# Routed experts: gate matmuls turned round, row scatters in one run, and another order of fetches and weight splits on ScalarE

## The reference

```
logits = einsum('bsh,he->bse', x, gate_w)
topv, topi = top_k(logits, 2)
w = softmax(topv, axis=-1)
w_e = einsum('bske,bsk->bse', one_hot(topi, 8), w)
out = einsum('bsh,eho,bse->bso', x, expert_w, w_e)
x = x + out
```

## Time and profile before

| | |
|---|---|
| runs | 1197.5, 1197.85, 1200.87 us; median 1197.85 us |
| profiled execution | 1197.45 us, its span 1195.6 us |
| TensorE busy | 1056.4 us (88%) |
| TensorE weight loads busy | 856.5 us (72%) |
| VectorE busy | 716.7 us (60%) |
| ScalarE busy | 359.7 us (30%) |
| GpSimd busy | 528.7 us (44%) |
| mean granted TensorE clock | 0.902 of full |

### The profile page before, as it was taken

How to read it: one execution, slowest core, us unless ns; L and a number is a source line. 1 busy time by engine, 2 the same in 40 slices (tenths; PEclk the granted TensorE clock), 3 DMA queues, 4 the chain that set the end, 5 groups by cost and what they waited for, 6 DMA issues and landing times. The chain is left out here.

```text
span 1195.6 us, 23715 instructions
## 1 busy us (share of the span) xinstructions
PE 1056.4 (88%) x8870; PEld 856.5 (72%) x8870; DVE 716.7 (60%) x1535; ACT 359.7 (30%) x828; POOL 528.7 (44%) x569
## 2 busy tenths in 40 slices
PE   6677766799999978999999999999999999873993
PEld 3344444688888767888888888888888887662782
DVE  5789999554444467566556556556656666640424
ACT  3544553222222233222222222222222222312331
POOL 0655666133213345545445444544544442045545
PEclk9767775699999988999999999999999999855997
DMA  8980000312101012110101101110110000035767
GB/s 313 394 268 2 0 2 2 76 46 75 53 26 47 27 35 63 48 34 28 53 28 46 36 27 45 29 52 27 27 54 27 28 10 1 26 131 184 219 199 251
DMA packets 61601, 90.88 MB, mean 76 GB/s; under 512 B 10376, under 2 KB 23944, under 8 KB 61512
## 3 DMA queue, kind: packets, MB, share of 16 engines
q1 hardware_dynamic: 51912, 68.09, 17.9%
q10 hardware_dynamic: 6624, 12.06, 3.1%
q0 software_dynamic: 2976, 9.44, 2.5%
HBM read 54.45 MB, written 35.13 MB: 75 GB/s over the span
## 5 line engine op out<-in xcount | busy, mean ns | idle before, releaser
L115 PE MATMUL PS<-NTh,W 128*128 128x256 f32 (+2 forms) x688 | 216.7, 315 | 0.0
L116 PE MATMUL PS<-NTl,W 128*128 128x256 f32 (+2 forms) x688 | 213.9, 311 | 0.0
L117 PE MATMUL PS<-NTh,W 128*128 128x256 f32 (+2 forms) x688 | 213.8, 311 | 0.0
L116 PEld LDWEIGHTS PS<-NTl,W 128*128 128x128 f32 (+1 forms) x688 | 131.2, 191 | 7.0
L117 PEld LDWEIGHTS PS<-NTh,W 128*128 128x128 f32 (+1 forms) x688 | 129.2, 188 | 8.5
L115 PEld LDWEIGHTS PS<-NTh,W 128*128 128x128 f32 (+1 forms) x688 | 129.4, 188 | 7.1
L1433 POOL TENSOR_TENSOR W<-ca_raw,W 128x512 fp32r<-128x512 f32 x64 | 82.5, 1291 | 114.8 <-ACT W L1283 114.8
L1371 DVE TENSOR_REDUCE ca_su<-room 128x4 f32<-128x256 f32 x64 | 26.9, 420 | 155.4 <-ACT room L1299 155.4
L1400 DVE TENSOR_TENSOR room<-PS,ca_sinT 64x512 f32<-64x512 f32 (+1 forms) x192 | 115.1, 600 | 2.6
L115 PE MATMUL PS<-W,ca_aTh 128*128 128x512 f32 x256 | 108.1, 422 | 3.2 <-DVE X L1388 3.1
L117 PE MATMUL PS<-W,ca_aTl 128*128 128x512 f32 x256 | 102.4, 400 | 0.0
(11 more groups left out here) (236 smaller groups left out, 2429.6 us busy)
## 6 DMA issues: line engine op xcount, KB each, us to landing
slots<-wa_blank SPq DMA_DIRECT2D x8, 2048.0 KB, 19.3
ca_raw<-in_L_Wq SPq DMA_DIRECT2D x32, 256.0 KB, 2.7
ca_raw<-in_L_Wo SPq DMA_DIRECT2D x32, 256.0 KB, 2.6
rf_raw<-in_experts SPq DMA_DIRECT2D x28, 256.0 KB, 3.2
outs<-wa_blank SPq DMA_DIRECT2D x1, 5888.0 KB, 31.2
room<-slots ACTq DMA_DIRECT2D x23, 256.0 KB, 3.2
outs<-room ACTq DMA_DIRECT2D x23, 256.0 KB
room<-in_L_Wg SPq DMA_DIRECT2D x10, 256.0 KB, 2.7
```

The lines of the kernel that those rows point to most:

```text
L115: nc.tensor.matmul(out, l_hi, r_hi, start=first, stop=False)
L116: nc.tensor.matmul(out, l_hi, r_lo, start=False, stop=False)
L117: return nc.tensor.matmul(out, l_lo, r_hi, start=False, stop=last)
```

## The change

Three things, all in `routed_ffn`.

1. **Logits.** The gate columns (8 wide) become the stationary operand and the tokens move: for the first four tiles 12 matmuls of 512 columns into an 8 x 512 result, for tiles 4 and 5 12 of 256, for `LATE` 12 of 256. ScalarE copies each 8-row result to SBUF (`logits_out`, line 1688 of the changed kernel), and TensorE turns it back, one 8-column transpose a tile (`by_token`, line 1606). TensorE's order becomes: logits of `EARLY`, transposes of the late norm tiles, turn back `EARLY`, logits of `LATE`, ranks of `EARLY`, turn back `LATE`, ranks of `LATE`. VectorE makes the low parts of the late norm tiles ahead of `choose(EARLY)` instead of behind it.
2. **GpSimd.** All 16 scatters come first, then the low parts of experts 1, 2 and 3.
3. **ScalarE.** High parts of expert 1, wait for the scatters, three fetches, high parts of expert 2, then the tile loop, with the high parts of expert 3 inside tile 0 and the exponential at the end of tile 2.

```diff
--- before.py
+++ after.py
@@ -1502,6 +1502,7 @@
     EARLY, LATE = range(TT - 2), range(TT - 2, TT)
     CHUNKS = EXPERTS * EC
     XR, RAW = 3, 4
+    PAIR = 2 * P
     HELD = TT + RAW
     with ExitStack() as st:
         sb, sem = allocator(nc, st)
@@ -1549,8 +1550,10 @@
         free_at = sb("rf_free_at", [P, EXPERTS], I32)
 
         T = [sh.PS[:, 0, :], sh.PS[:, 1, :]]
+        lgT = xr[0:EXPERTS, 0:2, :]
+        LGT = [[(sh.PS[0:EXPERTS, 2, :], 0, 0), (sh.PS[0:EXPERTS, 3, 0:PAIR], 1, 0)], [(sh.PS[0:EXPERTS, 7, 0:PAIR], 1, PAIR)]]
         LG, RK = ([sh.PS[:, first + step, 0:TT * EXPERTS].rearrange("p (t e) -> p t e", e=EXPERTS) for step in (0, 2)]
-                  for first in (2, 3))
+                  for first in (4, 3))
         TOTAL = sh.PS[:, 6, 0:EXPERTS]
         D = sh.PS[:, 4:8, :]
         raw_loaded = [sem(f"rf_raw{x}") for x in range(RAW)]
@@ -1558,7 +1561,7 @@
         fetched = [sem(f"rf_fetched{x}") for x in range(HELD)]
         held = norm.rows + [raw[:, x, :] for x in range(RAW)]
         kept = [sem(f"rf_kept{x}") for x in range(YR)]
-        names = ("lg_mm found merged rank_mm slot_ready scattered chain weighed planned w_hi w_split x_tr x_hi x_lo d_mm "
+        names = ("lgt_mm lgt_copied lg_mm found merged rank_mm slot_ready scattered chain weighed planned w_hi w_split x_tr x_hi x_lo d_mm "
                  "y_copied stored combined table_loaded").split()
         S = {x: sem("rf_" + x) for x in names}
 
@@ -1589,13 +1592,20 @@
 
             @block.tensor
             def _(pe):
-                def logits(tiles):
+                def logits(late):
+                    for out, half, start in LGT[late]:
+                        tok = slice(half * 4 * P + start, half * 4 * P + start + out.shape[-1])
+                        for c in range(EC):
+                            last = mm3(nc, out, gw[0][:, c, :], gw[1][:, c, :], sh.NTh[:, c, tok], sh.NTl[:, c, tok],
+                                       c == 0, c == EC - 1)
+                        last.then_inc(S["lgt_mm"], 1)
+
+                def by_token(tiles):
+                    pe.wait_ge(S["lgt_copied"], 2 if tiles is EARLY else 3)
                     for t in tiles:
-                        tok = slice(t * P, (t + 1) * P)
-                        for c in range(EC):
-                            last = mm3(nc, LG[tiles is LATE][:, t, :], sh.NTh[:, c, tok], sh.NTl[:, c, tok],
-                                       gw[0][:, c, :], gw[1][:, c, :], c == 0, c == EC - 1)
-                        last.then_inc(S["lg_mm"], 1)
+                        last = nc.tensor.transpose(LG[tiles is LATE][:, t, :], lgT[:, t // 4, t % 4 * P:(t % 4 + 1) * P],
+                                                   ident[0:EXPERTS, 0:EXPERTS])
+                    last.then_inc(S["lg_mm"], len(tiles))
 
                 def ranks(tiles):
                     some = slice(tiles[0], tiles[-1] + 1)
@@ -1610,12 +1620,14 @@
                             [P, some.stop - t - 1, EXPERTS]), start=False, stop=t == tiles[-2])
                     last.then_inc(S["rank_mm"], 1)
 
-                logits(EARLY)
+                logits(0)
+                norm.several_by_tensor(pe, LATE, T)
+                by_token(EARLY)
+                pe.wait_ge(norm.low_done, TT + 1)
+                logits(1)
                 pe.wait_ge(S["table_loaded"], 16)
-                norm.several_by_tensor(pe, LATE, T)
                 ranks(EARLY)
-                pe.wait_ge(norm.low_done, TT + 1)
-                logits(LATE)
+                by_token(LATE)
                 ranks(LATE)
                 for k, part in enumerate((sofar[:], both[:, TT - 2, :], both[:, TT - 1, :])):
                     last = nc.tensor.matmul(TOTAL, one, part, start=k == 0, stop=k == 2)
@@ -1670,17 +1682,22 @@
                     act.wait_ge(S["y_copied"], j + 1)
                     act.dma_start(d["outs"][j * P:(j + 1) * P, :], yr[:, j % YR, :]).then_inc(kept[j % YR], 16)
 
+                def logits_out(late):
+                    for out, half, start in LGT[late]:
+                        act.wait_ge(S["lgt_mm"], 2 * late + half * (1 - late) + 1)
+                        nc.scalar.activation(lgT[:, half, start:start + out.shape[-1]], out, ACT.Copy).then_inc(S["lgt_copied"], 1)
+
                 for t in LATE:
                     norm.root(act, t, t % 2)
+                logits_out(0)
                 for t in LATE:
                     norm.high(act, t, T[t % 2])
-                for e in (1, 2, 3):
-                    expert_high(e)
-                act.wait_ge(S["weighed"], 1)
-                nc.scalar.activation(e2[:], e2[:], ACT.Exp).then_inc(S["weighed"], 1)
+                logits_out(1)
+                expert_high(1)
                 act.wait_ge(S["scattered"], 32 * TT)
                 for j in range(XR):
                     fetch(j)
+                expert_high(2)
                 for j in range(SLOT_TILES):
                     act.wait_ge(S["x_tr"], j + 1)
                     if j >= TT:
@@ -1691,6 +1708,11 @@
                         fetch(j + XR)
                     if j >= 1:
                         keep(j - 1)
+                    if j == 0:
+                        expert_high(3)
+                    if j == 2:
+                        act.wait_ge(S["weighed"], 1)
+                        nc.scalar.activation(e2[:], e2[:], ACT.Exp).then_inc(S["weighed"], 1)
                 keep(SLOT_TILES - 1)
 
             @block.gpsimd
@@ -1711,11 +1733,10 @@
 
                 nc.gpsimd.memset(spare[:, 0:1], 0.0).then_inc(S["w_split"], EC)
                 nc.gpsimd.memset(spare[:, 1:2], 0.0).then_inc(S["d_mm"], 1)
-                expert_low(1)
                 scatter(EARLY)
-                expert_low(2)
                 scatter(LATE)
-                expert_low(3)
+                for e in (1, 2, 3):
+                    expert_low(e)
                 for e in range(RING, EXPERTS):
                     gp.wait_ge(S["planned"], 1)
                     done = gp.value_load(free_at[0:1, e - RING:e - RING + 1], min_val=1, max_val=SLOT_TILES + 1)
@@ -1778,12 +1799,12 @@
                     nc.vector.tensor_copy(slot[:, some, :], slotf[:, some, :]).then_inc(S["slot_ready"], 1)
 
                 norm.pair_by_vector(vec, LATE)
+                for t in LATE:
+                    norm.low(vec, t, T[t % 2])
                 vec.wait_ge(S["table_loaded"], 16)
                 choose(EARLY, 0, 0)
                 vec.wait_ge(S["merged"], TT - 2)
                 nc.vector.reduce_sum(sofar[:], both[:, 0:TT - 2, :].rearrange("p t e -> p e t"), AX_X).then_inc(S["merged"], 1)
-                for t in LATE:
-                    norm.low(vec, t, T[t % 2])
                 give_slots(EARLY, 3, 1)
                 choose(LATE, 6, 2 * len(EARLY))
                 give_slots(LATE, 9, 2)
```

## The result

| | before | after |
|---|---|---|
| median (lowest to highest) | 1197.5 us (1196.6 to 1200.87), 5 runs | 1189.97 us (1188.52 to 1191.32), 5 runs |
| ratio, 95% interval | | 0.9934 (0.9919 to 0.9949) |
| profiled execution, its span | 1197.45 us, 1195.6 us | 1189.97 us, 1188.1 us |
| mean granted TensorE clock | 0.902 | 0.905 |
| TensorE busy | 1056.4 us | 1052.8 us |

The change is faster by 7.5 us; 1188.5 was predicted, in a range from 1184.5 to 1193.5. Over all the profiles of this study B lies between 1040.0 and 1045.0 although nothing ahead of it differs, and the tail behind the first gather varies too; the distance from B to the first gather in one profile is therefore the sharper number.

A forecast was written before the change was run, and what follows sets the result against it. The last block was read as a string of stages each waiting for the last, up to the tile loop. Terms -5.6 - 1.65 - 4.8 + 1.2 + 1.5 = -9.35 us gave 1188.5 us, range 1184.5 to 1193.5.

The forecast's parts named there:

- Logits: From the first gate matmul to VectorE's copy of the logits: wide matmuls let the copy start 5.6 us earlier.
- The rival that the clock falls as before: TensorE drops to 1.2 GHz during the early logits; start only 4.1 us earlier, 1190.0 us; chance 0.28.
- Ranks: TensorE's rank matmuls: kept at 2.73 us, half clock, no gain; 1.4 us as the other bound.
- Slots: VectorE between ranks and first scatter: product and cast faster without GpSimd's splits, 1.65 us saved (bounds 0 and 1.8).
- Splits out of the scatters: GpSimd's four weight splits no longer between the 12th and 13th scatter: the last scatter's issue ends 4.8 us earlier still.
- First stand: ScalarE waits in expert 2's high parts for the last chunk, delaying tile 0: +1.2 us (bounds +0.2 and +1.7).
- rival of slow loads: Weight chunks take 6.5 us to land in both rounds, tile 1 starts 6.3 us later: 1193.6 us; chance 0.12.
- The second stand: ScalarE waits in expert 3's high parts ahead of tile 1; at 3.3 us landings hidden, with 1.3 us to spare.
- The exponential: Table load and exponential on ScalarE ahead of tile 3's high part: +1.5 us (bounds +0.6 and +1.5).
- The last sentence of the prediction: Wrong if ScalarE stands much longer in expert 2's or 3's high parts, or a rigidly moved loop stage stretches.
- The drain: At ScalarE's table load, the skill's extra drain: 1.4 us more, 1189.9 us; chance 0.02.
- Behind tile 6: The loop behind tile 5 and the gathers keep their distances: 0 from tile 6 to the first gather.

The follow-up runs named there:

- gate_only: The changed kernel with GpSimd's and ScalarE's old order, keeping the new logits: 1189.16 us, ratio 0.9933 against the kernel before.
- gate_ahead: gate_only with the exponential, compact_slots and weigh moved ahead of the tile loop: 1188.29 us, ratio 0.9919 against the kernel before.
- both_ahead: The changed kernel with the exponential, compact_slots and weigh moved ahead of the tile loop: 1183.28 us, ratio 0.989 against the kernel before.
- exp_early: The changed kernel with the exponential and its table load moved ahead of the wait for the scatters: 1184.58 us, ratio 0.9891.
- pool_waits: The changed kernel with GpSimd starting experts 4 to 7 only after tile 4's low part: 1183.78 us, ratio 0.9891.
- order_only: The kernel before, old logits kept, with GpSimd's and ScalarE's streams in the new order: 1196.3 us, ratio 0.9995.
- low_behind: both_ahead with the late tiles' low parts behind choose(EARLY) and late logits behind the early ranks: 1182.51 us, ratio 0.9879.

## Why the prediction was right, and where it was not

**Logits: right.** -5.6 forecast, -5.85 measured, and the order of the steps was as told: early logits over at B+4.17, copy of the logits at B+6.64 (forecast B+6.9). The rival that the clock falls as before did not happen: the granted clock was 1.00 through the whole stretch. With 8 stationary columns and 512 or 256 moving ones TensorE kept 2.4 GHz where, as busy but with 8 moving columns, it had fallen to 1.2. That a busy engine stays at 2.4 GHz, as the Trainium skill has it in TensorE: Matmul & The Clock Gate, Part 1: The HAM clock gate, agrees with the profile after and not with the one before.

**Ranks: kept at half clock, wrong by 1.25 us.** The reason was that TensorE stands idle much of this stretch; it did, for 1.11 and 0.81 us, and the clock stayed. The other bound, 1.4 us, was the value (1.48).

**Slots: right**, -1.76 for -1.65. gate_only shows the cause: 1.05 and 0.83 us beside splits, 0.26 and 0.17 without.

**Splits out of the scatters: right**, -4.82 for -4.8, and 16 scatters 1.27 us apart.

**First stand: +1.2 forecast, within its bounds; +1.7 measured** between gate_ahead and both_ahead from tile 2 on. At tile 0 it is more: the last chunk of expert 2 took 5.28 us to land, where 3.3 was taken and 4.1 was the highest in the earlier trace rows, as the chain of waits after shows:

```profile
1080.86 5.28 DMA rf_raw<-in_experts
```

So the rival of slow loads came halfway true. Tile 0 began 2.5 us later from E than before, and part of it was won back, since tile 0 ran less of its work at half clock: 5.2 us from tile 0's first matmul to tile 1's, where it had been 6.0. The second stand was nearly hidden, but without the 1.3 us to spare: tile 1's first matmul comes 0.64 us behind the start of the transposes ahead of it, where it is 0.36 at tile 2, so it waited some 0.3 us for its low part, which ended 0.15 us ahead of it.

**The exponential: the step that failed.** It was the term "with its small operations between, so no slack takes it up", +1.5 us with bounds of +0.6 and +1.5. That ScalarE is what tile 3 waits for held, and so did the duration, 1.41 us; the size was 5.4 us by the medians of exp_early and the change and 4.9 by their distances from E to tile 6, of which 0.5 comes at tile 3, 3.6 at tile 4 and 0.7 at tile 5. By itself the exponential costs 0.5 us (pool_waits), so TensorE's slack of 0.9 us, which the prediction took for its lower bound, did take up the rest; all beyond that is the string. What was missing is in the earlier trace rows themselves: the prediction read there that a product and a cast are four to five times as long beside GpSimd's splits, took 1.65 us for it at the slots, and moved `compact_slots` rigidly without asking what GpSimd does from tile 3 on. The answer is in the earlier trace rows: GpSimd began expert 4 at 1110.35, released by TensorE's last matmul of expert 0, tile 2, and the timeline of DVE before shows the string there:

```profile
1109.26 0.20 DVE L1834 TENSOR_TENSOR rf_sooner<-rf_table,rf_ends 128x48 f32<-128x48 f32 x1
...
1112.77 1.22 DVE L1857 CAST rf_out_slot<-rf_ordered 128x16 int32<-128x16 f32 x1
```

The string began 1.09 us ahead of GpSimd. Six of its operations were over when GpSimd began and the seventh 0.03 us later; four of the other seven were stretched already (0.70, 0.61, 0.58 and 1.22 us), and the string took 4.7 us. In the change it begins 0.28 us behind GpSimd (1100.09 and 1099.81). The last sentence of the prediction names this as a way to be wrong, but gives it no price and no rival.

The drain that the Trainium skill adds to a table load (ScalarE: Activation LUTs, What ACT_TABLE_LOAD costs) does not show here: the load is 1.28 us, the exponential begins 0.02 us behind it and tile 3's high part 1.41 us after the load's start.

**Behind tile 6: 0 forecast, -2.1 measured.** The first gather follows the store that it waits for at different distances. Chain of waits, before:

```profile
1161.40 3.73 DMA outs<-room
```

and gate_only:

```profile
1156.45 2.06 DMA outs<-room
```

The first gather starts 0.78 us behind the landing. Counted back by that, order_only, the other kernel with the old logits, has 3.3, and all eleven with the new ones 2.1; from tile 6 to the first gather it is 43.9 us before, 43.0 in order_only and 41.8 in the eleven. No run here tells why a store 110 us after the gate lands over 1 us sooner; it stays open. The same store is waited for in both, and the stores are issued 3.2 us apart in both.

## What to carry to other kernels

A delay on one engine is priced by what it pushes the next engine's work into, not by its own length: list what GpSimd does at the new time of each moved VectorE operation. Strings of small VectorE operations belong where GpSimd only issues DMAs or is idle; here a one-tile move of such a string, or one wait on GpSimd, gave 7.6 and 6.2 us by the medians (4.5 and 6.7 us by the distance from B to the first gather) on top of the 7.5 of the whole change. And where a long reordering measures nothing (ratio 0.9995 for order_only), look for the stage that gives it back: 6.5 us were there ahead of E, and 6.7 were returned behind it, 2.0 by tile 2 and 4.7 at tiles 3 to 5.

## What the runs showed of the hardware that was not expected

- Beside GpSimd's splits and casts of weights (512 elements a partition, 1.26 us each for a split) VectorE's small products, casts and scalar operations with operands in SBUF mostly took 0.36 to 1.36 us instead of 0.15 to 0.29, whatever their size: a cast of 6 elements 1.23, a product of 128 1.25. Reductions (0.21 and 0.29 us), the reciprocal (0.20) and the low parts, which read PSUM (0.69), kept their times. Under the casts of expert 4 (0.6 us each) they took 0.36 to 0.72, under the splits (1.26 each) mostly 0.98 to 1.36. The rows of the change show what each waits for: GpSimd has eight instructions there, four casts and four splits, and the eight stretched operations of the string end one behind each of them, 0.01 to 0.15 us after its end (for the splits, ends at 1103.35, 1104.57, 1105.78 and 1107.05 against 1103.38, 1104.65, 1105.93 and 1107.08). In the trace this wait is busy time of the VectorE row, with no idle time and no releaser. The Trainium skill, SBUF — State Buffer, Who interferes with whom, says the same as a rule: VectorE instructions with two SBUF inputs, and casts, copies and scalar operations where they use a second port, share that port with GpSimd, whoever is first holds it for a whole instruction, and reductions never contend. The rows agree on each kind (1.36 and 1.25, 1.23 for the cast, 0.29 for the reduction, 0.69 where one input is in PSUM).
- Beside indirect DMAs issued by GpSimd this did not happen (0.22 and 0.29 in both_ahead, the string 2.4 us); at most a single row was longer by 0.2 us (a scalar operation on `rf_row`, 0.38 before and 0.18 after).
- The clock stayed at 2.4 GHz through idle times of 1.11 and 0.81 us. After one of 4.48 us it did not fall while TensorE stood (granted 1.00 from 1103.5 to 1108.2), but 0.8 us into tile 4 (0.97 from 1108.26 to 1109.0, 0.55 from 1109.1 to 1112.7, 1.00 from 1112.7 on). In low_behind it fell about 1 us into the ranks, behind an idle time of 2.63 us.
- The tail from the first gather to the end lay between 28.5 and 31.1 us in 13 profiles in which nothing there differs, and B between 1040.0 and 1045.0; both are larger than several of the effects above, so those rest on distances inside the block.
